# A quantised feed-forward taken chunk by chunk, with its weights turned inside the layer norm ahead of it

## The chip, the cores and the metric

The kernel runs as one program on one core of a Trainium2 chip. The metric is the device time of one execution in microseconds, where less is better. A core has TensorE (matrix products; PE in the rows, PEld for its weight loads), VectorE (DVE), ScalarE (ACT), GpSimd (POOL) and SyncE (SP), which issues the transfers. Each engine runs its own instructions in order, and the engines wait for each other by semaphores.

## The reference, cut to what matters

Two blocks of a perceiver (cross-attention, self-attention, feed-forward) on x of 2 x 256 rows and 256 columns. The changed part is the last: a layer norm and a feed-forward whose weights are quantised to 4 bits in blocks of 32 and whose activations are quantised to 16 bits over the whole tensor. Each `act_qdq` needs the largest absolute value of the entire tensor before its first element can be rounded.

```python
def act_qdq(x):
    scale = jnp.maximum(jnp.max(jnp.abs(x)) / qmax, 1e-12)     # qmax = 32767
    return jnp.clip(jnp.round(x / scale), -qmax - 1.0, qmax) * scale
def fixed_qdq_u16(x):
    scale = 1.0 / 65536.0
    return jnp.clip(jnp.round(x / scale), 0.0, 65535.0) * scale
x = act_qdq(x)                                  # 512 rows x 256
up = act_qdq(x @ lpbq_dequant(w_up).T)          # 512 x 768
gate = act_qdq(x @ lpbq_dequant(w_gate).T)
sig = fixed_qdq_u16(jax.nn.sigmoid(gate))
gate = act_qdq(gate * sig)
o = act_qdq(gate * up)
return o @ lpbq_dequant(w_down).T
# and: x = x + ffn(layernorm(x))
```

## The kernel before

The program is a sequence of blocks. At the end of a block all engines meet, so the next block's first instruction on any engine comes after the previous block's last on every one. Inside a block the order on each engine is the order of the code.

The last two blocks are `layer_norm(chip, "ln5")` and `quantised_ffn`. The layer norm takes statistics of the 512 rows (4 tiles of 128) on VectorE, a power of -0.5 on GpSimd (L155), normalises on VectorE (L147) into `xn`, and turns `xn` on TensorE into `xnT` (2 x 128 partitions x 512 columns), whose halves VectorE and ScalarE (L169) copy out of PSUM.

`quantised_ffn` holds the 768 hidden units as 6 chunks of 128 partitions x 512 columns, side by side as 3072 columns of `gate`, `up` and `sg`. Its work on each engine:

- TensorE turns the three weight matrices (36 transposes of 128 x 128, L2112), then makes 6 gate chunks and 6 up chunks (L2123) in four PSUM banks in turn, and at the end the down product (L2130): 4 tiles of rows, each summed over the 6 chunks before the next tile begins.
- ScalarE copies the turned weights to SBUF (L2138), each chunk of gate and up to SBUF (L2141), then takes the sigmoid of all 3072 columns and its rounding.
- VectorE finds the maxima (L2064 by chunk, L2067 over the six; L2070, L2081, L2087), makes the scales from one column (L2046, L2047), and rounds. Rounding is adding the constant MAGIC = 12582912.0 in float32, and taking it away in a later instruction:

```python
def rounded(t, src, factor):
    link(dve.tensor_scalar(t, src, factor, MAGIC, ALU.mult, ALU.add))                # L2051
    link(dve.tensor_scalar(t, t, MAGIC + QM, MAGIC - QM - 1.0, ALU.min, ALU.max))    # L2052
```

- GpSimd spreads each of the five maxima over the partitions by `partition_all_reduce` (L2102). These five are its only work there. The dequantising of the weights (`DequantisedWeights.work`) was done on GpSimd beside the self-attention before the layer norm.
- SyncE stores the four tiles of the output as VectorE finishes them (L2096).

Names: `f_am` are the maxima per partition, `f_ar` those over all partitions, `f_sc` the scales, `f_rc` their reciprocals, `dq_w` the dequantised weights. `a_all` and `o_all` are two PSUM banks each, `s_all` is four.

Of the kernel before, what the change touches and what calls it, by code (L numbers as in the profile page):

```python
# [10 lines left out]
F32 = mybir.dt.float32  # L11
# [7 lines left out]
P = 128  # L19
# [99 lines left out]
def layer_norm(chip, tag, after=()):  # L119


    nc = chip.nc
    with ExitStack() as scope:
# [6 lines left out]
        with nc.Block() as block:  # L130
# [6 lines left out]
            def _(dve):  # L137
# [20 lines left out]
            def _(pe):  # L158
                pe.wait_ge(xn_done, NT)
# [1791 lines left out]
class DequantisedWeights:  # L1951
# [3 lines left out]
    def __init__(self, chip, tag, scope, mats, outs):  # L1955
# [6 lines left out]
        self.loaded, self.step, self.scaled = (chip.sem(f"{tag}_{n}") for n in ("ld", "step", "scaled"))  # L1962
# [14 lines left out]
    def loads(self, sp):  # L1977
        for i in range(3):
            sp.dma_start(self.flat(i), self.mats[i].rearrange("(o p) c -> p o c", p=P)).then_inc(self.loaded, 16)

# [32 lines left out]
def quantised_ffn(chip, tag, dequantised, upT, gateT, downT, out_dram):  # L2013
# [3 lines left out]
    QM = 32767.0  # L2017
    with ExitStack() as scope:
# [4 lines left out]
        am = chip.sb(f"{tag}_am", [P, 5], F32, scope)  # L2023
        cm = chip.sb(f"{tag}_cm", [P, 2 * I6], F32, scope)
        magic = chip.sb(f"{tag}_magic", [P, 1], F32, scope)
        cmd, magic_set = chip.sem(f"{tag}_cmd"), chip.sem(f"{tag}_magic")
        ar = chip.sb(f"{tag}_ar", [P, 5], F32, scope)
        sc = chip.sb(f"{tag}_sc", [P, 5], F32, scope)
        rc = chip.sb(f"{tag}_rc", [P, 5], F32, scope)
        st, amd, ard, mm, ev, sgd, dn, out, qd = (chip.sem(f"{tag}_{x}") for x in ("st", "amd", "ard", "mm", "ev", "sgd", "dn", "out", "qd"))  # L2030
        stored, tr, tro = chip.sem(f"{tag}_stored"), chip.sem(f"{tag}_tr"), chip.sem(f"{tag}_tro")
        with nc.Block() as block:
            @block.vector
            def _(dve):
                n = 0

                def link(ins):
                    nonlocal n
                    n += 1
                    ins.then_inc(st, 1)  # L2040
                    dve.wait_ge(st, n)

                def scale(i, factor=1.0 / QM):

                    dve.wait_ge(ard, i + 1)
# [3 lines left out]
                def rounded(t, src, factor):  # L2049

                    link(dve.tensor_scalar(t, src, factor, MAGIC, ALU.mult, ALU.add))  # L2051
                    link(dve.tensor_scalar(t, t, MAGIC + QM, MAGIC - QM - 1.0, ALU.min, ALU.max))  # L2052

                def qdq(i, t, src):

                    scale(i)
                    rounded(t, src, rc[:, i:i + 1])
                    dve.tensor_scalar(t, t, MAGIC, sc[:, i:i + 1], ALU.subtract, ALU.mult).then_inc(qd, 1)  # L2058

                def chunk_maxima(first):  # L2060

                    for n in range(first, first + I6):
                        dve.wait_ge(ev, n + 1)
                        dve.tensor_reduce(cm[:, n:n + 1], (gate if n < I6 else up)[:, n % I6, :], AX.X, ALU.max, apply_absolute_value=True).then_inc(cmd, 1)  # L2064
                    dve.wait_ge(cmd, first + I6)
                    i = 1 + first // I6
                    dve.tensor_reduce(am[:, i:i + 1], cm[:, first:first + I6], AX.X, ALU.max).then_inc(amd, 1)  # L2067

                dve.memset(magic[:], MAGIC).then_inc(magic_set, 1)
                dve.tensor_reduce(am[:, 0:1], chip.xnT[:], AX.XY, ALU.max, apply_absolute_value=True).then_inc(amd, 1)  # L2070
# [5 lines left out]
                dve.wait_ge(qd, 3)  # L2076

                dve.wait_ge(sgd, 2)
                link(dve.tensor_scalar(sg[:], sg[:], MAGIC + 65535.0, MAGIC, ALU.min, ALU.max))  # L2079
                link(dve.scalar_tensor_tensor(out=gate[:], in0=sg[:], scalar=MAGIC, in1=gate[:], op0=ALU.subtract, op1=ALU.mult))  # L2080
                dve.tensor_reduce(am[:, 3:4], gate[:], AX.XY, ALU.max, apply_absolute_value=True).then_inc(amd, 1)  # L2081
                scale(3, 2.0 ** -16 / QM)
                link(dve.tensor_scalar(rc[:, 3:4], rc[:, 3:4], 2.0 ** -16, None, ALU.mult))
                rounded(gate[:], gate[:], rc[:, 3:4])

                link(dve.scalar_tensor_tensor(out=gate[:], in0=gate[:], scalar=MAGIC, in1=up[:], op0=ALU.subtract, op1=ALU.mult))
                dve.tensor_reduce(am[:, 4:5], gate[:], AX.XY, ALU.max, apply_absolute_value=True).then_inc(amd, 1)  # L2087
                dve.wait_ge(ard, 5)
# [216 lines left out]
```

## Time and profile before

| | |
|---|---|
| median of 3 runs | 1759.65 us (1758.5 to 1762.81) |
| the profiled execution's time, and its span | 1759.81 us, 1758.0 us |
| TensorE, VectorE, ScalarE, GpSimd busy | 1562.5, 1132.3, 875.0, 685.5 us |
| last layer norm | from 1668.72 to 1675.94 us of the span |
| weight transposes and xq | to 1685.42 us |
| gate and up products | to 1708.0 us |
| element-wise work, TensorE idle | to 1742.80 us |
| down product | to 1755.4 us |
| last sum and store | to 1758.0 us |

The span runs from the first instruction to the end of the last; the time holds some 2 us around it. Busy shares over the span say little about the tail, which is the only part that the change touches; that part is read by its timeline.

### The profile page before, as it was taken

The numbers are of one execution on the slowest core, as the hardware profiler recorded it, in microseconds if no ns is written. First come the engines' busy times: TensorE is split into PE (matmuls) and PEld (weight loads), VectorE is DVE, ScalarE is ACT, GpSimd is POOL, SyncE is SP. The second block draws the span as 40 slices with busy tenths as digits, with TensorE's granted clock in tenths as the row PEclk, the third lists the DMA queues.
The fourth block names the chain that finished last, engine by engine and source line by source line (L and its number), as shares of the span: only waits on it lengthen the run. The fifth ranks groups of instructions, "written<-read, shape, count | busy, mean of one in ns | idle before, by whom it ended". The sixth has DMA issues, their size and how long they took to land. (4 is left out here: it accounts for less than half of the span.)

```text
span 1758.0 us, 42136 instructions
## 1 busy us (share of the span) xinstructions
PE 1562.5 (89%) x15980; PEld 882.6 (50%) x15980; DVE 1132.3 (64%) x1756; ACT 875.0 (50%) x1178; POOL 685.5 (39%) x535
## 2 busy tenths in 40 slices
PE   3999999999499999999777958999999999967772
PEld 1455455455133333333453426777777777753442
DVE  4665665665499999997337747666666666425356
ACT  2555555555167777778251014555555555523440
POOL 2431000000111111111053108999999999933500
PEclk9999999999689999999798969999999999988886
DMA  4787988888432222221300057565546555012000
GB/s 162 199 216 226 223 216 221 222 231 211 146 101 68 65 65 65 65 65 34 153 1 1 1 138 217 152 158 149 146 124 164 145 153 155 27 35 91 1 0 12
DMA packets 178076, 212.14 MB, mean 121 GB/s; under 512 B 57080, under 2 KB 151428, under 8 KB 173342
## 3 DMA queue, kind: packets, MB, share of 16 engines
q1 hardware_dynamic: 177376, 210.37, 43.3%
q8 instruction: 91, 1.49, 0.4%
q14 instruction: 33, 0.27, 0.1%
q10 hardware_dynamic: 576, 0.00, 0.0%
HBM read 122.71 MB, written 87.57 MB: 120 GB/s over the span
## 5 line engine op out<-in xcount | busy, mean ns | idle before, releaser
L1121 POOL TENSOR_TENSOR x_r<-x_p 128x1024 f16<-128x1024 f32 x256 | 479.0, 1893 | 24.0 <-ACT x_p L1097 16.9
L1136 DVE TENSOR_REDUCE x_mx<-a_all 128x2 f32<-128x1024 f32 x249 | 304.9, 1224 | 147.2 <-PE a_all L1020 147.2
L1097 ACT ACTIVATE x_p<-s_all 128x1024 f32<-128x1024 f32 x256 | 248.4, 1022 | 223.1 <-PE s_all L1003 223.1
L702 ACT ACTIVATE x_p<-s_all 128x1024 f32<-128x1024 f32 x256 | 261.0, 1023 | 49.2 <-PE s_all L612 41.9
L757 DVE TENSOR_REDUCE x_mx<-a_all 128x1 f32<-128x512 f32 x352 | 229.9, 684 | 16.7 <-PE o_all L623 8.7
L1003 PE MATMUL s_all<-x_q,x_k 64*128 64x256 f16 x3072 | 210.0, 269 | 0.0
L1038 PEld LDWEIGHTS o_all<-x_v,x_p 128*128 128x128 bf16 x2048 | 178.7, 97 | 40.1 <-issue 40.1
L1038 PE MATMUL o_all<-x_v,x_p 128*128 128x129 f16 x2048 | 197.3, 221 | 0.9 <-POOL x_r L1121 0.9
L1039 PE MATMUL o_all<-x_v,x_r 128*128 128x65 f16 x2048 | 192.5, 193 | 0.0
L1039 PEld LDWEIGHTS o_all<-x_v,x_r 128*128 128x128 f16 x2048 | 180.7, 98 | 0.0
L1003 PEld LDWEIGHTS s_all<-x_q,x_k 64*128 64x128 f16 x3072 | 149.4, 94 | 62.2 <-issue 0.8
L651 PE MATMUL o_all<-x_p,x_vf 128*32 128x256 f32 x2048 | 163.3, 392 | 1.1 <-ACT x_osb L691 1.1
L623 PE MATMUL a_all<-x_k,x_qa 64*128 64x512 f16 x352 | 124.4, 396 | 25.3 <-DMA x_v<-values 22.1
L716 POOL MEMSET x_k<- 128x2048 f16 x2 | 3.6, 1804 | 318.2 <-POOLq L265 318.2
L731 POOL TENSOR_TENSOR x_mcol<-x_nm,x_zero 128x4 f16<-128x4 f32 x32 | 6.8, 213 | 304.8 <-DVE x_nm L764 304.8
L757 DVE TENSOR_REDUCE x_mx<-o_all 128x1 f32<-128x512 f32 x160 | 109.7, 686 | 4.3 <-PE a_all L623 0.5
L1020 PE MATMUL a_all<-x_k,x_q 64*128 64x512 f16 x498 | 97.4, 388 | 13.9 <-DVE x_mx L1136 7.3
L612 PE MATMUL s_all<-x_qb,x_k 64*128 64x256 f16 x1024 | 103.2, 277 | 0.0
L997 PE MATMUL s_all<-x_qm,x_ones 64*128 64x512 f16 x512 | 99.9, 387 | 0.0
L395 DVE TENSOR_TENSOR vst<-a_all,vst 128x512 f16<-128x512 f32 (+1 forms) x96 | 57.9, 603 | 41.4 <-ACT vst L363 40.7
L395 DVE TENSOR_TENSOR vst<-o_all,vst 128x512 f16<-128x512 f32 (+1 forms) x96 | 57.8, 603 | 41.5 <-ACT vst L363 41.0
L612 PEld LDWEIGHTS s_all<-x_qb,x_k 64*128 64x128 f16 x1024 | 30.0, 94 | 104.7 <-issue 82.0
(347 smaller groups left out, 2784.1 us busy)
## 6 DMA issues: line engine op xcount, KB each, us to landing
values<-vst SPq DMA_DIRECT2D x16, 2064.0 KB, 10.3
x_v<-values SPq DMA_DIRECT2D x32, 1032.0 KB, 5.2
keys<-kst SPq DMA_DIRECT2D x32, 1024.0 KB, 6.5
x_k<-keys SPq DMA_DIRECT2D x128, 256.0 KB, 5.1
x_k<-keys SPq DMA_DIRECT2D x192, 64.0 KB, 2.1
values<-vst SPq DMA_DIRECT2D x16, 528.0 KB, 11.5
x_v<-values SPq DMA_DIRECT2D x32, 264.0 KB, 2.6
cf<-in_ctxT SPq DMA_DIRECT2D x16, 512.0 KB, 9.5
```

Of the source, the lines that this page charges most:

```text
L395: dve.tensor_tensor(lo, src, hi, ALU.subtract).then_inc(lo_done, 1)
L612: last = pe.matmul(chip.s_ps[g % 2][:, c * SQ:(c + 1) * SQ], kbuf[w][r, (2 * g + j) * P:(2 * g + j + 1) * P], qb[w][r, :], start=True, sto ...
L623: pe.matmul(bank(place)[:], qa[w][r, qt * P:(qt + 1) * P], kbuf[w][r, c * 512:(c + 1) * 512], start=True, stop=True).then_inc(chunk_ready, 1)
L651: last = pe.matmul(o[32 * c:32 * c + 32, 0:SQ], vf[w][:, kt, :], prob[g % NP][:, c, :], start=(g == 0), stop=(g == GR - 1), skip_group_che ...
L702: act.activation(prob[g % NP][:], chip.s_ps[g % 2][:].rearrange("p (c q) -> p c q", q=SQ), ACT.Exp, scale=hd ** -0.5).then_inc(p_ready, 1)
L757: dve.tensor_reduce(mx[a[1] % 2][:, n // 8, n % 8:n % 8 + 1], bank(place)[:], AX.X, ALU.max).then_inc(chunk_done, 1)
L1003: last = pe.matmul(s[:, c * SQ:(c + 1) * SQ], k[w][kp][r, (2 * g + j) * P:(2 * g + j + 1) * P], q[w][qp][r, :], start=False, stop=(kp == 1 ...
L1038: pe.matmul(o[:, qt * VC:(qt + 1) * VC], hi, v[w][:, kt, :], start=begin, stop=False, skip_group_check=True)
L1039: last = pe.matmul(o[:, qt * VC:qt * VC + 1 + hd], rest[i][:, c, qs], v[w][:, kt, 0:1 + hd], start=False, stop=end, skip_group_check=True)
L1097: act.activation(prob[g % NP][:], chip.s_ps[g % 2][:].rearrange("p (c q) -> p c q", q=SQ), ACT.Exp, scale=hd ** -0.5).then_inc(p_ready, 1)
L1121: pool.tensor_tensor(rest[g % NP][:], prob[g % NP][:], hi, ALU.subtract).then_inc(rest_done, 1)
L1136: dve.tensor_reduce(mx[a[1] % 2][:, n // 4, 2 * (n % 4):2 * (n % 4) + 2], chunk_banks(u, g)[:, :].rearrange("p (h c) -> p h c", h=2), AX.X ...
```

## The change

The changed feed-forward works on chunks of 512 columns throughout:

- The weight transposes and their copies move into the layer norm (`turned`), ahead of the transposes of `xn` on TensorE and of the copy of `xnT` on ScalarE. GpSimd calls one idle all-reduce and then that of the first maximum there (`scales`); this maximum is now taken of `xn`, before it is turned.
- The gate chunks stay in PSUM (banks 0 to 5, the up chunks in banks 6, 7 and 0 to 3). VectorE takes maxima there, and ScalarE's rounding (an Identity activation with scale `rc` and bias MAGIC) brings them to SBUF.
- ScalarE does all rounding of gate, silu, up and the product, by chunks; the clips of the five `act_qdq` go (only the sigmoid's upper one stays). VectorE subtracts MAGIC and multiplies. For chunks 0 to 3 ScalarE also subtracts MAGIC from the rounded sigmoid, for 4 and 5 VectorE.
- The down product runs over chunks outside and over row tiles inside, so it needs one chunk at a time.

```diff
@@ layer_norm, VectorE, GpSimd, TensorE, ScalarE
+                if scales is not None:
+                    dve.wait_ge(xn_done, NT)
+                    dve.tensor_reduce(scales.am[:, 0:1], chip.xn[:], AX.XY, ALU.max, apply_absolute_value=True).then_inc(scales.found, 1)
...
                 pool.tensor_tensor(rs[:], ve[:], chip.half[:, 0:NT], ALU.pow).then_inc(rstd, 1)
+                if scales is not None:
+                    pool.partition_all_reduce(scales.idle[:], chip.half[:, 0:1], P, bass.bass_isa.ReduceOp.absmax)
+                    scales.over_rows(pool, 0)
...
+                if turned is not None:
+                    turned.turn(pe)
                 pe.wait_ge(xn_done, NT)
...
+                if turned is not None:
+                    turned.keep(act)
                 act.wait_ge(tr, 2)
@@ quantised_ffn, VectorE
-                qdq(0, xq[:], chip.xnT[:])
-                chunk_maxima(0)
-                qdq(1, gate[:], gate[:])
-                chunk_maxima(I6)
-                qdq(2, up[:], up[:])
...
+                scale(0)
+                for k in range(KT):
+                    link(dve.tensor_scalar(xq[:, k, :], chip.xnT[:, k, :], rc[:, 0:1], MAGIC, ALU.mult, ALU.add))
+                    dve.tensor_scalar(xq[:, k, :], xq[:, k, :], MAGIC, sc[:, 0:1], ALU.subtract, ALU.mult).then_inc(x_done, 1)
+                for m in range(I6):
+                    dve.wait_ge(gate_ready, m + 1)
+                    chunk(0, m, gate_bank[m])
+                largest(1, 0, I6)
+                scale(1)
+                dve.sem_inc(scale_done, 1)
+                for m in range(I6):
+                    gate_back(m)
+                    if m in (1, 3, 5):
+                        up_max(m // 2)
+                silu_max(0)
+                up_max(3)
+                silu_chunk(0)
+                for m in range(1, 4):
+                    silu_max(m)
+                    if m < 3:
+                        up_max(3 + m)
+                    silu_chunk(m)
+                    if m == 2:
+                        largest(2, 1, 2 * I6 + 3)
+                scale(2)
+                dve.sem_inc(scale_done, 1)
+                for m in range(4, I6):
+                    whole(m)
+                    silu_max(m)
+                    silu_chunk(m)
+                largest(3, 2, 3 * I6)
+                for m in range(4):
+                    up_back(m)
...
+                for m in range(4, I6):
+                    up_back(m)
+                product(0)
+                for m in range(1, I6):
+                    product(m)
+                    product_chunk(m - 1)
+                product_chunk(I6 - 1)
+                largest(4, 3, 4 * I6)
...
+                link(dve.tensor_scalar(gate[:, 0, :], gate[:, 0, :], rc[:, 4:5], MAGIC, ALU.mult, ALU.add))
+                for m in range(I6):
+                    if m:
+                        dve.wait_ge(down_round, m)
+                    dve.tensor_scalar(gate[:, m, :], gate[:, m, :], MAGIC, sc[:, 4:5], ALU.subtract, ALU.mult).then_inc(down_done, 1)
@@ quantised_ffn, TensorE: the down product
+                for k in range(I6):
+                    pe.wait_ge(down_done, k + 1)
+                    for t in range(NT):
                         last = pe.matmul(chip.banks[t][:, 0:D], gate[:, k, t * P:(t + 1) * P], downT[:, k, :],
@@ quantised_ffn, ScalarE
-                act.activation(sg[:], gate[:], ACT.Sigmoid).then_inc(sgd, 1)
...
+                def rounded(out, src, i, done):
+                    act.activation(out, src, ACT.Identity, bias=magic[:, 0:1], scale=rc[:, i:i + 1]).then_inc(done, 1)
...
+                act.activation(warm[:], magic[:, 0:1], ACT.Sigmoid)
+                act.wait_ge(scale_done, 1)
+                for m in range(I6):
+                    rounded(gate[:, m, :], gate_bank[m], 1, gate_round)
+                for m in range(I6):
+                    sigmoid(m)
+                    sigmoid_round(m)
+                    if m < 4:
+                        sigmoid_whole(m)
+                act.wait_ge(scale_done, 2)
+                for m in range(I6):
+                    rounded(up[:, m, :], up_bank[m], 2, up_round)
+                act.wait_ge(scale_done, 3)
+                for m in range(I6):
+                    rounded(silu[:, m, :], silu[:, m, :], 3, silu_round)
+                act.wait_ge(scale_done, 4)
+                for m in range(1, I6):
+                    rounded(gate[:, m, :], gate[:, m, :], 4, down_round)
```

GpSimd in the last two blocks, before: the power of the layer norm, a branch into the feed-forward's block, and there the all-reduces, the first with an instruction without operands ahead of it (both print as ISA).

```order
L155 TENSOR_TENSOR ln_rs<-ln_ve,half 128x4
L130 UNCONDITIONAL_BRANCH
L2098 UNCONDITIONAL_BRANCH
L2102 ISA
L2102 ISA f_ar<-f_am 128x1 x5
```

The same place of the changed kernel:

```order
L157 TENSOR_TENSOR ln_rs<-ln_ve,half 128x4
L159 ISA
L159 ISA f_idle<-half 128x1
L2046 ISA f_ar<-f_am 128x1
L129 UNCONDITIONAL_BRANCH
L2194 UNCONDITIONAL_BRANCH
L2046 ISA f_ar<-f_am 128x1 x4
```

The instruction without operands and the first all-reduce of a maximum now stand ahead of the branch, inside the layer norm.

VectorE from the silu product to the last scale, before:

```order
L2080 SCALAR_TENSOR_TENSOR f_gate<-f_sg,f_gate 128x3072
L2081 TENSOR_REDUCE f_am<-f_gate 128x1
L2046 TENSOR_SCALAR f_sc<-f_ar 128x1
L2047 RECIPROCAL f_rc<-f_sc 128x1
L2083 TENSOR_SCALAR f_rc<-f_rc 128x1
L2051 TENSOR_SCALAR f_gate<-f_gate,f_rc 128x3072
L2052 TENSOR_SCALAR f_gate<-f_gate 128x3072
L2086 SCALAR_TENSOR_TENSOR f_gate<-f_gate,f_up 128x3072
L2087 TENSOR_REDUCE f_am<-f_gate 128x1
```

VectorE of the changed kernel, from chunk 5 of silu to the second chunk of the product (the maxima of `f_cm` are over one chunk):

```order
L2114 TENSOR_SCALAR f_sg<-f_sg 128x512
L2109 SCALAR_TENSOR_TENSOR f_silu<-f_sg,f_gate 128x512
L2092 TENSOR_REDUCE f_cm<-f_silu 128x1
L2096 TENSOR_REDUCE f_am<-f_cm 128x1
L2122 TENSOR_SCALAR f_up<-f_up,f_sc 128x512 x4
L2087 TENSOR_SCALAR f_sc<-f_ar 128x1
L2088 RECIPROCAL f_rc<-f_sc 128x1
L2170 TENSOR_SCALAR f_rc<-f_rc 128x1
L2122 TENSOR_SCALAR f_up<-f_up,f_sc 128x512 x2
L2127 SCALAR_TENSOR_TENSOR f_gate<-f_silu,f_up 128x512 x2
L2092 TENSOR_REDUCE f_cm<-f_gate 128x1
```

The passes L2051 and L2052 over 3072 columns are gone from VectorE, four of the six instructions that scale `up` back stand between a maximum and its scale, and products and maxima alternate by chunk.

## Rows read from the trace of the kernel before

**Rows 1.** The page: head.

```profile
span 1758.0 us, 42136 instructions
```

**Rows 2.** The chain over 1660 to 1758 us: shares by line; pieces (start, us, what).

```profile
by line: issue 17.1%; PE a_all L2123 12.5%; PE o_all L2123 10.5%; PE a_all L2130 7.6%; PE o_all L2130 5.3%; DVE f_gate L2080 3.4%; DVE f_am L2081 3.4%; DVE f_up L2051 1.9%; DVE f_up L2058 1.9%; DVE f_gate L2051 1.9%; DVE f_gate L2093 1.9%; 
...
1742.80 7.43 PE a_all L2130 x24
1750.22 5.19 PE o_all L2130 x24
```

**Rows 3.** Timeline, last layer norm (start us, us, engine, line, operation).

```profile
1668.72 1.40 DVE L139 BATCH_NORM_STATS2 ln_st<-x 128x6 f32<-128x256 f32 x4 [0.51 <-PEq L1180]
...
1670.82 1.04 POOL L155 TENSOR_TENSOR ln_rs<-ln_ve,half 128x4 f32<-128x4 f32 x1 [12.21 <-DVE ln_ve L144]
1671.89 1.38 DVE L147 TENSOR_SCALAR xn<-x,ln_mv,ln_rs 128x256 f32<-128x256 f32 x4 [1.15 <-POOL ln_rs L155]
...
1675.34 0.60 ACT L169 ACTIVATE xnT<-a_all 128x512 f32<-128x512 f32 x1 [11.43 <-PE a_all L162]
```

**Rows 4.** Timeline, start of the feed-forward.

```profile
1676.24 6.97 PE L2112 MATMUL s_all<-ident,dq_w 128*128 128x128 f32 x36 [0.94 <-PEq L130]
...
1682.17 0.41 POOL L2102 PARTITION_ALL_REDUCE f_ar<-f_am  x1 [10.31 <-issue]
...
1683.00 0.75 DVE L2051 TENSOR_SCALAR f_xq<-xnT,f_rc 128x1024 f32<-128x1024 f32 x1
...
1684.52 0.76 DVE L2058 TENSOR_SCALAR f_xq<-f_xq,f_sc 128x1024 f32<-128x1024 f32 x1
...
1685.42 5.37 PE L2123 MATMUL a_all<-f_xq,gateT 128*128 128x512 f32 x8 [2.21 <-DVE f_xq L2058]
```

**Rows 5.** Timeline, the last gate chunk, its scale, the last up chunk.

```profile
1697.69 0.60 ACT L2141 ACTIVATE f_gate<-a_all 128x512 f32<-128x512 f32 x1 [1.12 <-PE a_all L2123]
...
1699.04 0.16 DVE L2067 TENSOR_REDUCE f_am<-f_cm 128x1 f32<-128x6 f32 x1
...
1699.88 0.16 DVE L2047 RECIPROCAL f_rc<-f_sc 128x1 f32<-128x1 f32 x1
...
1707.99 0.60 ACT L2141 ACTIVATE f_up<-o_all 128x512 f32<-128x512 f32 x1 [1.12 <-PE o_all L2123]
```

**Rows 6.** Timeline, VectorE to the end.

```profile
1705.46 3.84 DVE L2064 TENSOR_REDUCE f_cm<-f_up 128x1 f32<-128x512 f32 x6
...
1717.67 3.36 DVE L2080 SCALAR_TENSOR_TENSOR f_gate<-f_sg,f_gate 128x3072 f32<-128x3072 f32 x1
...
1732.52 3.35 DVE L2087 TENSOR_REDUCE f_am<-f_gate 128x1 f32<-128x3072 f32 x1
...
1736.98 0.16 DVE L2091 TENSOR_TENSOR f_rc<-f_rc,f_sc 128x1 f32<-128x1 f32 x1
...
1755.44 0.42 DVE L2096 TENSOR_TENSOR x<-o_all,x 128x256 f32<-128x256 f32 x1 [2.17 <-PE o_all L2130]
```

**Rows 7.** Groups by form: line, operation, count, busy us, mean ns, idle before.

```profile
L2064 DVE TENSOR_REDUCE f_cm<-f_gate 128x1 f32<-128x512 f32 x6 | 4.1, 686 | 9.6 <-ACT f_gate L2141 9.6
L2141 ACT ACTIVATE f_gate<-a_all 128x512 f32<-128x512 f32 x4 | 2.4, 597 | 8.6 <-PE a_all L2123 8.6
L361 ACT ACTIVATE kst<-o_all,bk 128x512 f16<-128x512 f32 x64 | 43.9, 686 | 34.9 <-PE o_all L336 34.9
L2093 DVE TENSOR_SCALAR f_gate<-f_gate,f_sc 128x3072 f32<-128x3072 f32 x1 | 1.8, 1820 | 0.0
```

**Rows 8.** Timeline of ScalarE in the last self-attention.

```profile
1607.81 0.59 ACT L1573 ACTIVATE s_hi<-a_all 128x512 f16<-128x512 f32 x1
1608.28 0.60 ACT L1577 ACTIVATE s_lo<-a_all 128x512 f16<-128x512 f32 x1
```

**Rows 9.** Busy time by stretch; the number after POOL's is TensorE's granted clock.

```profile
1685.40:1688.80 3.40, 3.38 (x4) 1.50 (x5) 0.00 (x0) 0.00 (x0) 0.00 (x0) 0.50 0.00 0
1688.80:1698.00 9.20, 9.20 (x23) 4.07 (x22) 3.43 (x5) 3.30 (x6) 0.00 (x0) 1.00 0.00 0
```

More of the change, by code:

```diff
@@ L1979, in loads, with turn, keep @@
             sp.dma_start(self.flat(i), self.mats[i].rearrange("(o p) c -> p o c", p=P)).then_inc(self.loaded, 16)
+    def turn(self, pe):
+        for n, (_i, _dst, srcs) in enumerate(self.jobs):
+            if n >= 4:
+                pe.wait_ge(self.kept, n - 3)
+            for a, src in enumerate(srcs):
+                last = pe.transpose(self.chip.banks[4 + n % 4][:, a * P:(a + 1) * P], src, self.chip.ident[:])
+            last.then_inc(self.tr, 1)
+    def keep(self, act):
+        for n, (_i, dst, srcs) in enumerate(self.jobs):
+            act.wait_ge(self.tr, n + 1)
+            act.activation(dst, self.chip.banks[4 + n % 4][:, 0:len(srcs) * P], ACT.Copy).then_inc(self.kept, 1)
     def scales(self, dve, i):
@@ L2017, in quantised_ffn @@
     QM = 32767.0
+    gate_bank = [chip.banks[m] for m in range(I6)]
+    up_bank = [chip.banks[(I6 + m) % 8] for m in range(I6)]
     with ExitStack() as scope:
@@ L2054, in qdq @@
[L2054 to L2067, printed above, removed]
@@ L2080, in _, with chunk, largest @@
[L2080 to L2081 removed]
+                def chunk(part, m, src):
+                    c = part * I6 + m
+                    dve.tensor_reduce(cm[:, c:c + 1], src, AX.X, ALU.max, apply_absolute_value=True).then_inc(chunk_max, 1)
+                def largest(i, part, total):
+                    dve.wait_ge(chunk_max, total)
+                    dve.tensor_reduce(am[:, i:i + 1], cm[:, part * I6:(part + 1) * I6], AX.X, ALU.max).then_inc(found, 1)
@@ new lines, in up_max, with gate_back, silu_max @@
+                def up_max(m):
+                    dve.wait_ge(up_ready, m + 1)
+                    chunk(1, m, up_bank[m])
+                def gate_back(m):
+                    dve.wait_ge(gate_round, m + 1)
+                    dve.tensor_scalar(gate[:, m, :], gate[:, m, :], MAGIC, sc[:, 1:2], ALU.subtract, ALU.mult).then_inc(gate_done, 1)
+                def silu_max(m):
+                    dve.wait_ge(sg_whole, m + 1)
+                    dve.wait_ge(gate_done, m + 1)
+                    dve.scalar_tensor_tensor(out=silu[:, m, :], in0=sg[:, m, :], scalar=65535.0, in1=gate[:, m, :],
+                                             op0=ALU.min, op1=ALU.mult).then_inc(silu_done, 1)
@@ new lines, in whole, with silu_chunk, up_back @@
+                def whole(m):
+                    dve.wait_ge(sg_round, m + 1)
+                    dve.tensor_scalar(sg[:, m, :], sg[:, m, :], MAGIC, None, ALU.subtract).then_inc(sg_whole, 1)
+                def silu_chunk(m):
+                    dve.wait_ge(silu_done, m + 1)
+                    chunk(2, m, silu[:, m, :])
+                def up_back(m):
+                    dve.wait_ge(up_round, m + 1)
+                    dve.tensor_scalar(up[:, m, :], up[:, m, :], MAGIC, sc[:, 2:3], ALU.subtract, ALU.mult).then_inc(up_done, 1)
@@ new lines, in product, with product_chunk @@
+                def product(m):
+                    dve.wait_ge(silu_round, m + 1)
+                    dve.wait_ge(up_done, m + 1)
+                    dve.scalar_tensor_tensor(out=gate[:, m, :], in0=silu[:, m, :], scalar=MAGIC, in1=up[:, m, :],
+                                             op0=ALU.subtract, op1=ALU.mult).then_inc(product_done, 1)
+                def product_chunk(m):
+                    dve.wait_ge(product_done, m + 1)
+                    chunk(3, m, gate[:, m, :])
+                dve.memset(magic[:, 0:1], MAGIC).then_inc(magic_set, 1)
@@ new lines, in _ @@
+                for m in range(I6):
+                    for k in range(KT):
+                        if m == 0:
+                            pe.wait_ge(x_done, k + 1)
+                        last = pe.matmul(gate_bank[m], gateT[:, k, m * P:(m + 1) * P], xq[:, k, :], start=(k == 0), stop=(k == KT - 1))
+                    last.then_inc(gate_ready, 1)
+                for m in range(I6):
+                    if m >= 2:
+                        pe.wait_ge(gate_round, m - 1)
+                    for k in range(KT):
+                        last = pe.matmul(up_bank[m], upT[:, k, m * P:(m + 1) * P], xq[:, k, :], start=(k == 0), stop=(k == KT - 1))
+                    last.then_inc(up_ready, 1)
```

118 lines of the change are left out of this document (51 added, 67 removed).

## The prediction

> **What bounds the kernel now.** I read the timeline first, to find where the changed code runs, then the chain of waits over it, then groups and stretches for prices. Nothing before the last layer norm is touched: the change can only move the time from about 1668.7 us to the end of the span at 1758.0 [rows 1]. In that tail almost nothing overlaps. The chain [rows 2] goes over long pieces of one engine after another: the two products with the gate and up weights (L2123, the parts named a_all and o_all), the down product (L2130) in two pieces of 7.43 and 5.19 us, and between them VectorE instructions over all 3072 columns. The reader should see in [rows 3, 4] that the layer norm ends with ScalarE's copy at 1675.34 + 0.60 = 1675.94, and that the first gate product starts only at 1685.42. GpSimd's first all-reduce (L2102) began at 1682.17, though its data came from a reduction that needed 1.2 us of the block: its idle time is put down to "issue", no engine. So something that belongs to this first call takes 1682.17 - 1676.24 = 5.93 us from the opening of the block, and xq waits for it. From the last gate chunk to its scale [rows 5] it is an eviction, a reduction and the all-reduce; then VectorE works alone until the down product at 1742.80, and TensorE stands still from 1708.0.
>
> **The prices of one chunk of 512 columns.** VectorE's reduction takes 0.686 us for 512 columns [rows 7] and 3.36 us for 3072 [rows 6], so a column costs 1.04 ns and the two-input instruction (3.36 us for 3072) comes to 0.69 us too. Six reductions in a row take 3.84 us [rows 6], 0.64 us each. A one-input instruction costs 0.752 us at 1024 columns [rows 4] and 1.82 us at 3072 [rows 7]: 0.52 ns a column, 0.48 us at 512, and I take 0.43 in a row. ScalarE takes 0.597 us, or 0.686 with a column operand [rows 7]; instructions that don't wait for each other start 0.47 us apart [rows 8], 0.12 less than they last; I take 0.11 less, so 0.58 us in a row with a column operand. A dependent instruction on another of these engines starts 0.03 us after its producer (1670.82 + 1.04 to 1671.89, [rows 3]), and TensorE 0.14 us after VectorE (1684.52 + 0.76 to 1685.42, [rows 4]).
>
> **Step 1, the start of the gate product.** The 36 weight transposes and their evictions move into the layer norm, ahead of xn's own eight on TensorE and ahead of xnT's copy on ScalarE. The first all-reduce, with an idle one before it, moves there as well, behind the power at L155. Three ends compete. GpSimd: the power ends at 1670.82 + 1.04 = 1671.86 [rows 3]; + 5.93, and two all-reduces of 0.41 [rows 4], gives 1678.61. TensorE and ScalarE: 36 transposes took 6.97 us [rows 4]; from 1668.72 they end at 1675.7, eight more at the same rate 1677.2, a copy of 0.60 gives 1677.9. VectorE has 1.2 us of reduction more behind 1673.3 and is done before that. So GpSimd ends the block, 2.7 us later than now. Then 0.30 us to the next block (1675.94 to 1676.24), 0.1 for two one-column memsets, 0.38 for two one-column operations, 0.48 + 0.03 + 0.48 for the first half of xq, 0.14 to TensorE: 1680.5. Before, 1685.42: **4.9 us** gained. The second half of xq comes 0.9 us later, while TensorE has 1.7 us or more of work on the first. TensorE's clock was 0.50 of full speed, 1.2 GHz, in the first 3.4 us of the product and 2.4 GHz after it [rows 9]; before the product it had stood still for 2.2 us. Now it stands still longer, so I keep the slow start.
>
> **Step 2, the gate scale.** Chunks stay in PSUM and VectorE reduces them there, so the eviction between product and reduction falls away: 1697.69 + 0.60 before the reduction starts [rows 5]. **0.65 us** with its gap.
>
> **Step 3, from the gate scale to the down product.** It took 1742.80 - 1700.04 = 42.76 us [rows 2, 5]. Now, with t = 0 at the gate scale:
> - To the up scale. ScalarE rounds six chunks, 0.03 + 0.69 + 5 x 0.58 = 3.62, then per chunk sigmoid, rounding and subtraction, each dependent: 0.60 + 0.69 + 0.69 + 0.06 = 2.04, and 1.93 in a row. The first whole chunk is there at 5.55. VectorE then has, per chunk, a product with the gate, an up maximum and a silu maximum: 3 x 0.64 = 1.93, the same pace. Three such rounds to 11.4, the small maximum 0.16, another product and maximum 1.4, two one-column operations 0.34: 13.25. The last up chunk is no limit: six chunks of (1707.99 - 1697.69)/6 = 1.72 us behind the gate's put it at 8.6, and its maximum has its turn at 10.1.
> - To the silu scale. Chunks 4 and 5 each 0.42 + 0.69 + 0.69 with gaps, 3.67; the small maximum 0.19; four one-input instructions 1.72; three one-column ones 0.5: 6.0.
> - To the last scale. 0.03 + 0.69 for ScalarE's first rounded chunk, then six products and six maxima on VectorE at 0.64, 7.7; with the small maximum and the same handing over as now, (1736.98 + 0.16) - (1732.52 + 3.35) = 1.27 [rows 6]: 10.0.
> - To TensorE: 0.48 + 0.48 + gaps + 0.14 = 1.2, one chunk instead of three passes.
> Together 30.4. I add 0.2 for four separate semaphore increments that VectorE now issues behind the scales (estimate, 0.05 each). **12.2 us** gained. Why it shrinks: four rounding passes over 3072 columns (L2051) leave VectorE for ScalarE, and four clipping passes (L2052) are gone.
>
> Here the Trainium skill speaks against the change: Perfetto Trace Analysis, Optimizing Scalar/DVE Operations, says that every VectorE or ScalarE instruction pays a fixed access cost, about 60 ns on VectorE from SBUF, so larger operations are better where the engine is full. The row bears out the direction with a larger size: six pieces in 3.84 us against one of 3.36 is 0.10 us for each extra instruction [rows 6]. By the page's figure the some 33 chunk instructions of this step on VectorE would take 1.3 us less than in my sum (estimate); I keep the row's.
>
> **Step 4, the end.** 48 products in 1755.44 - 1742.80 = 12.64 us [rows 2, 6], the slow clock at their start included. Chunk by chunk they can't be faster than now, but VectorE's chunks come every 0.48 to 0.58 us and TensorE needs at least 12.64/6 x 0.8 = 1.7 for one: no wait. The four sums now come in the last 1.3 us rather than one every 2.6, and so do the four stores: I take 0.3 us lost, between 0 (the last store starts no later) and 1.0.
>
> Sum: 4.9 + 0.65 + 12.2 - 0.3 = 17.4 us. The span becomes 1740.6; the profiled execution took 1759.81 around a span of 1758.0, so 1742.4, and as its time is within 0.2 us of the median of the runs, 1742.4 is the forecast, 1.0% faster.
>
> **Bounds.** If nothing pipelines (0.69 for each ScalarE and VectorE chunk instruction, dependent or not), step 3 takes 2.2 us more. If GpSimd's first call needs 1.2 us more, that goes to the block's end whole. If TensorE starts the gate product at 2.4 GHz, 1.9 us less (1685.42 + 5.4 for what takes 3.43 later). With the scatter of the three runs around their median, -1.2 to +3.2 us, I get 1739 to 1747.5; that is the forecast's own range too, and it holds the two milder rivals.
>
> **Rivals.**
> - ScalarE and VectorE wait for each other at each chunk, and the handing over costs more than 0.03 us; some 35 handings over in step 3 at 0.14 us, TensorE's price, would add 3.9 us: 1746.3. For it: the chain of now has few handings over, so 0.03 rests on few rows. Against it: those rows are of the same two engines. 13 in 100.
> - The layer norm takes it back. If the transposes hold up xn's, or the first call comes later, the block ends at 1681 and step 1 gives 2.5: 1744.8. Against it: 0.7 us of slack between the two ends. 8 in 100.
> - The change doesn't do what it says: the tail shrinks, but the other 1669 us of the span, whose code is the same, grow by 0.7% or more, as their instructions lie elsewhere in memory. No row shows such a thing. The time would be within 5.3 us of now (0.3%, about what a measurement of this kernel can tell from no change): 1757. 2 in 100.
> - Slower. TensorE stays at 1.2 GHz through gate, up and down products. The last up chunk then comes at 12 x 3.43 = 41.2 us behind the start, 17 us after VectorE's turn for it, and the down product takes 4 x 5.19 = 20.8 (24 of its 48 products took 5.19 at the end [rows 2]) instead of 12.6, 8.2 more: 1742.4 + 25 = 1767.6. From 17.4 us of lateness on it decides. For it: the clock was at 0.50 at the start of the same product, and TensorE stands still longer before it. Against it: the same unbroken row of products brought the clock to 1.00 after 3.4 us [rows 9]. 2 in 100. The Trainium skill, TensorE: Matmul & The Clock Gate, in its part on oscillation, describes bursts divided by waits that each start at the slow clock; by it the down product, now six bursts, would suffer if they were apart, and here none waits.
>
> The forecast's own mechanism has 75 in 100. Of all cases 96 in 100 are faster by over 0.3%, 2 within, 2 slower.
>
> **What the new profile would show.** In the layer norm GpSimd's last all-reduce ends at 1678.6 and is the last instruction of the block; the gate product starts at 1680.5; 14.0 us later ScalarE's first rounding; scales at +13.3, +6.0, +10.0 us; the down product at about 1724.9; ScalarE's instructions 0.58 us apart. VectorE and ScalarE both busy over 85% in between. Wrong would be: a start of the gate product after 1682, one-input instructions of over 0.55 us beside ScalarE, or gaps over 0.1 us at each chunk.

## The result, and the profile after

The changed kernel takes 1741.18 us (median of 4 runs, 1739.34 to 1743.06) against 1760.52 us for the kernel before beside it (4 runs, 1758.5 to 1762.81): a ratio of 0.9895, 95% interval 0.9882 to 0.9908, or 16.2 to 20.8 us. The forecast was 1742.4.

The profiled execution has a span of 1737.6 us. Its timeline in the last layer norm and at the opening of the feed-forward answers to [rows 3, 4] (start us, us, engine, line, operation):

```profile
1665.14 1.41 DVE L138 BATCH_NORM_STATS2 ln_st<-x 128x6 f32<-128x256 f32 x4 [0.51 <-PEq L1189]
1665.14 4.88 PE L1996 MATMUL s_all<-ident,dq_w 128*128 128x128 f32 x36 [0.98 <-PEq L1189]
...
1667.25 1.04 POOL L157 TENSOR_TENSOR ln_rs<-ln_ve,half 128x4 f32<-128x4 f32 x1 [11.90 <-DVE ln_ve L143]
...
1670.94 0.60 ACT L178 ACTIVATE xnT<-a_all 128x512 f32<-128x512 f32 x1 [0.30 <-PE a_all L169]
1674.22 0.41 POOL L159 PARTITION_ALL_REDUCE f_idle<-half  x1 [5.94 <-issue]
1674.55 0.43 POOL L2046 PARTITION_ALL_REDUCE f_ar<-f_am  x1
1675.29 1.28 ACT L2240 ACT_TABLE_LOAD   x1 [3.76 <-PEq L129]
...
1676.84 6.01 PE L2205 MATMUL a_all<-f_xq,gateT 128*128 128x512 f32 x8 [5.94 <-DVE f_xq L2139]
```

GpSimd's idle call starts 5.94 us after the end of the power (1667.25 + 1.04), idle time that the profile puts down to "issue", and the block ends with the all-reduce at 1674.98, while ScalarE's last copy was done at 1671.54: 3.4 us of the block are the first call alone. The statistics begin at 1665.14, 3.58 us earlier in the span than before, in code that is the same; the experiments come back to this. So the stages are compared by their distances, not by their places.

VectorE and ScalarE from the gate scale on, and the end (answering to [rows 5, 6]):

```profile
1691.31 0.16 DVE L2088 RECIPROCAL f_rc<-f_sc 128x1 f32<-128x1 f32 x1
1691.57 1.45 ACT L2225 ACTIVATE f_gate<-a_all,f_magic,f_rc 128x512 f32<-128x512 f32 x2 [14.78 <-DVEq L2145]
...
1705.35 0.16 DVE L2088 RECIPROCAL f_rc<-f_sc 128x1 f32<-128x1 f32 x1
...
1709.42 1.67 DVE L2122 TENSOR_SCALAR f_up<-f_up,f_sc 128x512 f32<-128x512 f32 x4
...
1711.18 0.16 DVE L2088 RECIPROCAL f_rc<-f_sc 128x1 f32<-128x1 f32 x1
...
1711.63 4.34 ACT L2225 ACTIVATE f_silu<-f_silu,f_magic,f_rc 128x512 f32<-128x512 f32 x6 [1.26 <-DVEq L2171]
...
1721.15 0.16 DVE L2183 TENSOR_TENSOR f_rc<-f_rc,f_sc 128x1 f32<-128x1 f32 x1
...
1722.61 2.05 PE L2217 MATMUL a_all<-downT,f_gate 128*128 128x256 f32 x4 [22.59 <-DVE f_gate L2189]
...
1734.44 0.85 DVE L2192 TENSOR_TENSOR x<-o_all,x 128x256 f32<-128x256 f32 x2
```

Busy time by stretch of the changed kernel, answering to [rows 9] (PE, PEld, DVE, ACT, POOL, then the granted clock):

```profile
1691.50:1722.60 31.10, 8.52 (x20) 3.44 (x19) 27.45 (x59) 24.01 (x36) 1.85 (x3) 0.72 0.00 1
1676.84:1680.80 3.96, 3.96 (x5) 1.85 (x6) 0.97 (x3) 0.00 (x0) 0.00 (x0) 0.50 0.00 0
1680.80:1690.00 9.20, 9.20 (x22) 3.94 (x21) 3.57 (x6) 0.00 (x0) 0.00 (x0) 0.96 0.00 0
```

Between the gate scale and the down product VectorE is busy 88% and ScalarE 77% of the time. The gate product begins at 1.2 GHz again (0.50). The mean of 0.96 in the next stretch says that the rise came some 0.7 us into it, so the slow start lasts 4.6 us instead of 3.4. Groups by form, answering to [rows 7]:

```profile
L2225 ACT ACTIVATE f_silu<-f_silu,f_magic,f_rc 128x512 f32<-128x512 f32 x6 | 4.3, 802 | 1.3 <-DVEq L2171 1.3
L2233 ACT ACTIVATE f_sg<-f_sg,f_magic 128x512 f32<-128x512 f32 x6 | 4.3, 722 | 0.2
L2109 DVE SCALAR_TENSOR_TENSOR f_silu<-f_sg,f_gate 128x512 f32<-128x512 f32 x6 | 4.2, 692 | 1.2 <-ACT f_sg L2237 0.8
```

The distances, in us, one profiled execution each (the gate scale is the end of its reciprocal; the down product runs to the end of the span):

| stage | before | forecast | after |
|---|---|---|---|
| first statistics to the gate product's start | 16.70 | 11.8 | 11.70 |
| gate product's start to the gate scale | 14.62 | 13.97 | 14.63 |
| gate scale to the down product's start | 42.76 | 30.6 | 31.14 |
| down product's start to the end | 15.20 | 15.5 | 14.99 |
| sum | 89.28 | 71.9 | 72.46 |

### The profile page after: what moved, and what is told of

It is laid out like the page before. It is cut to its first block and busy times, and to the rows that moved or that the text cites. A ratio compares the mean times of both kernels' runs of the same rounds, so it can differ in the third digit from the quotient of the medians.

```text
span 1737.6 us, 42209 instructions
## 1 busy us (share of the span) xinstructions
PE 1554.7 (89%) x15980; PEld 876.2 (50%) x15980; DVE 1120.5 (64%) x1789; ACT 888.9 (51%) x1204; POOL 687.4 (40%) x536
## 5 line engine op out<-in xcount | busy, mean ns | idle before, releaser
L1029 PE MATMUL a_all<-x_k,x_q 64*128 64x512 f16 x498 | 97.4, 388 | 14.3 <-DVE x_mx L1145 7.3
```

## The experiments

All were profiled and timed beside the kernel before, the first four together, the next four together, the last by itself. "Tail" is the distance from the last layer norm's first statistics to the end of the span, in the profiled execution.

| kernel | median us | ratio to before | statistics start at | to gate product | to gate scale | to down product | to end | tail |
|---|---|---|---|---|---|---|---|---|
| a_turn_only | 1759.60 | 1.0009 | 1665.80 | 15.78 | 15.77 | 42.76 | 15.69 | 90.00 |
| b_first_reduce_only | 1759.26 | 0.9994 | 1667.20 | 16.87 | 12.94 | 42.77 | 15.82 | 88.40 |
| c_down_by_tile | 1748.30 | 0.9937 | 1666.44 | 11.65 | 14.67 | 34.22 | 15.02 | 75.56 |
| d_no_early_table | 1745.55 | 0.9929 | 1665.81 | 11.44 | 14.91 | 32.65 | 16.09 | 75.09 |
| after_again | 1743.31 | 0.9903 | 1670.78 | 11.61 | 14.83 | 31.14 | 15.14 | 72.72 |
| e_clock_kept | 1738.77 | 0.9879 | 1670.24 | 11.61 | 12.38 | 31.62 | 13.35 | 68.96 |
| f_early_first_call | 1741.30 | 0.9896 | 1673.30 | 8.97 | 12.38 | 31.14 | 14.91 | 67.40 |
| g_both | 1734.52 | 0.9856 | 1668.63 | 9.21 | 12.38 | 31.16 | 13.32 | 66.07 |
| h_chunk3_on_vector | 1735.52 | 0.9872 | 1667.32 | 9.21 | 12.39 | 31.46 | 13.42 | 66.48 |

**Each move into the layer norm alone.** Both start from the kernel before. a_turn_only takes the transposes and their copies into the layer norm:

```diff
             def _(pe):
+                if turned is not None:
+                    turned.turn(pe)
                 pe.wait_ge(xn_done, NT)
...
             def _(act):
+                if turned is not None:
+                    turned.keep(act)
```

> The kernel before, with only the weight transposes and their copies moved into the layer norm. My theory: the start of the gate product was bound by GpSimd's first all-reduce (5.93 us from the block's opening), so moving the transposes alone gives nothing: the gate product starts 13.6 us after the end of the power on GpSimd, as before, and the time is 1760.5 us, within 1 us. Rival: the transposes (6.97 us) bound it: the gate product starts some 4 us earlier, 1756.

b_first_reduce_only takes the idle all-reduce and the first maximum there:

```diff
                 pool.tensor_tensor(rs[:], ve[:], chip.half[:, 0:NT], ALU.pow).then_inc(rstd, 1)
+                if scales is not None:
+                    pool.partition_all_reduce(scales.idle[:], chip.half[:, 0:1], P, bass.bass_isa.ReduceOp.absmax)
+                    scales.over_rows(pool, 0)
```

> The kernel before, with only the idle all-reduce and that of the first maximum moved into the layer norm; the transposes stay in the feed-forward. My theory: the block of the layer norm ends 2.7 us later and the transposes then take their 7.0 us, so the gate product starts 14.1 us after the power instead of 13.6: 1761, within 1 us of before or a little slower; the two moves pay only together (5.0 us). Rival: the first call was the only bound, and this move alone brings the 5 us: 1755.5.

Neither is told from before: ratios 1.0009 (0.9996 to 1.0021) and 0.9994 (0.9982 to 1.0006). The timeline of a_turn_only shows what holds its gate product up:

```profile
1671.60 0.60 ACT L173 ACTIVATE xnT<-a_all 128x512 f32<-128x512 f32 x1 [0.29 <-PE a_all L164]
...
1678.43 0.41 POOL L2120 PARTITION_ALL_REDUCE f_ar<-f_am  x1 [9.49 <-issue]
...
1681.58 6.51 PE L2134 MATMUL a_all<-f_xq,gateT 128*128 128x512 f32 x8 [10.02 <-DVE f_xq L2076]
```

The layer norm is over at 1672.20 and all weights are turned, but the first all-reduce starts 6.2 us later, and TensorE waits for xq. In b_first_reduce_only the all-reduce is out of the way, and the transposes are in it:

```profile
1676.58 0.43 POOL L2029 PARTITION_ALL_REDUCE f_ar<-f_am  x1
...
1677.36 6.04 PE L2126 MATMUL s_all<-ident,dq_w 128*128 128x128 f32 x36 [3.58 <-PEq L130]
...
1684.07 3.70 PE L2137 MATMUL a_all<-f_xq,gateT 128*128 128x512 f32 x8 [0.67 <-ACT downT L2152]
```

Here the product's releaser is ScalarE's copy of the turned weights. The start comes 0.9 us earlier than before in one and 0.2 later in the other; in the changed kernel it is 5.0 us earlier. Two works of 6 to 7 us stood side by side, and each covered the other. Not all of the 5.0 us is the two moves, though. In b_first_reduce_only xq, still made whole and with its clip, is ready 12.85 us after the first statistics:

```profile
1679.30 0.75 DVE L2074 TENSOR_SCALAR f_xq<-f_xq,f_sc 128x1024 f32<-128x1024 f32 x1
```

With 0.14 us to TensorE the two moves alone would start the product at 13.0 (estimate), 3.7 us earlier than before. The other 1.3 us come from xq in halves and without its clip. No run has the two moves alone.

A detail in the same rows: the first eight matmul records take 6.51 us where TensorE had waited 10.02 us, and 3.70 us where it came straight from the transposes. In before it was 5.37 us, in the changed kernel 6.01.

**The order of the down product.** c_down_by_tile is the changed kernel with

```diff
-                for k in range(I6):
-                    pe.wait_ge(down_done, k + 1)
-                    for t in range(NT):
+                pe.wait_ge(down_done, I6)
+                for t in range(NT):
+                    for k in range(I6):
```

> The changed kernel, with the down product again over row tiles outside and chunks inside, waiting for all six chunks. My theory: it starts when the sixth chunk is ready, 2.95 us later than in the changed kernel, less 0.3 us that the spread stores give back: 1741.2 + 2.7 = 1743.9. Rival: the product's slow start at 1.2 GHz hides the order, and the time stays at 1741.2.

```profile
1726.98 7.22 PE L2217 MATMUL a_all<-downT,f_gate 128*128 128x256 f32 x24 [25.67 <-DVE f_gate L2189]
...
1739.42 0.42 DVE L2192 TENSOR_TENSOR x<-o_all,x 128x256 f32<-128x256 f32 x1 [2.17 <-PE o_all L2217]
```

The down product starts 34.22 us after the gate scale instead of 31.14, 3.1 us later. From its start to the end it takes 15.02 us, as in the changed kernel (14.99), but that sum hides two small differences. From the end of the last addition to the end of the span it takes 2.16 us (1742.0 - 1739.84) against 2.31 in the changed kernel (1737.6 - 1735.29); over all profiles it is 2.07 to 2.16 us where the tiles end 2.6 us apart and 2.31 to 2.36 where they end together. So the spread stores do give back 0.15 us, half of what was expected. And the product's slow start lasted 3.7 us here against 3.3. The tail is 3.1 us longer (2.8 against after_again). The rival falls. The medians differ by 5 us (from after_again) to 7, more than the tail of the one profiled execution explains; the rest may lie ahead of the layer norm, where nothing was changed, but only one execution was profiled, the fastest of the four.

**The table load.** d_no_early_table leaves out the one-column sigmoid:

```diff
-                act.activation(warm[:], magic[:, 0:1], ACT.Sigmoid)
```

> The changed kernel without the one-column sigmoid at the opening of the feed-forward. My theory: the table load of 1.28 us then falls between ScalarE's rounding of the gate and its first sigmoid, on the path to the up scale, which ScalarE paces: 1741.2 + 1.3 = 1742.5. Rival: VectorE paces that stretch and hides it: 1741.2.

ScalarE's timeline shows the load where it was expected:

```profile
1694.98 1.46 ACT L2225 ACTIVATE f_gate<-s_all,f_magic,f_rc 128x512 f32<-128x512 f32 x2
1696.46 1.28 ACT L2229 ACT_TABLE_LOAD   x1
1697.76 0.63 ACT L2229 ACTIVATE f_sg<-f_gate 128x512 f32<-128x512 f32 x1
```

Gate scale to down product is 32.65 instead of 31.14, 1.5 us more, the load with what it displaces. The rest of the tail's 2.6 us is not the load's: 0.3 in the gate product and 1.1 from the down product on, whose slow start lasted 5.3 us here and 3.3 in the changed kernel.

**The changed kernel again.** No edit.

> The changed kernel once more, unaltered, as the measure for the three kernels run beside it. My theory: the last layer norm's first statistics to the end of the span take 72.5 us again, within 1.5 us for where TensorE's clock rises; the time of the part ahead of it, whose code is that of before, scatters by some us from execution to execution (it was 1668.7 and 1665.1 us in the two first profiles). Rival: the part ahead is shorter in the changed kernel for good, by some 2 us.

Every distance in the tail repeats within 0.2 us; the statistics begin 5.6 us later than in its first profile. Over all eleven profiles, whose code is the same up to there but for GpSimd's first call in three of them, that start lies between 1665.1 and 1673.3 us. The rival, a part ahead that is shorter for good, is not borne out. Two stretches ahead of the tail, the first pair of the first profile, the second of after_again:

```profile
480.00:500.00 20.00, 17.95 (x71) 4.56 (x70) 19.52 (x35) 6.31 (x7) 3.07 (x6) 0.57 0.33 88
500.00:520.00 20.00, 19.73 (x220) 7.42 (x216) 18.55 (x35) 15.85 (x18) 1.53 (x3) 1.00 0.45 131
```

```profile
480.00:500.00 20.00, 18.19 (x63) 4.67 (x67) 19.52 (x35) 6.42 (x7) 2.81 (x6) 0.50 0.32 88
500.00:520.00 20.00, 19.73 (x208) 6.98 (x200) 17.32 (x31) 14.31 (x17) 1.80 (x4) 0.92 0.44 130
```

TensorE is busy for the same share of both, but its clock rises later in the second, and it gets through 271 records there instead of 291. By the two means the lower clock lasts 6.0 us longer in the second, which is worth 3.0 us at most of the 5.6 (estimate). So it goes with a part of the longer time; that it is the cause of the scatter was not shown. Of the four executions timed beside after_again the median is 15.8 us below before's (14.2 to 20.1 us by the interval, 0.9886 to 0.9919), against 19.3 the first time.

**The clock.** e_clock_kept adds idle transposes that nobody reads:

```diff
+                    pe.wait_ge(turned.kept, len(turned.jobs))
+                    for n in range(32):
+                        pe.transpose(chip.banks[4 + n % 4][:, 0:P], chip.ident[:], chip.ident[:])
...
+                for n in range(12):
+                    pe.transpose(chip.banks[7][:, 0:P], chip.ident[:], chip.ident[:])
                 for m in range(I6):
...
                 pe.wait_ge(up_round, I6)
+                for n in range(90):
+                    pe.transpose(chip.banks[7][:, 0:P], chip.ident[:], chip.ident[:])
```

> The changed kernel with idle transposes on TensorE: 32 behind those of xn, 12 ahead of the gate product, 90 ahead of the down product, into PSUM banks that nobody reads. My theory: both products then start at 2.4 GHz. From the gate product's start to the gate scale 12.0 instead of 14.6 us, from the down product's start to its last sum 10.4 instead of 12.3: 72.5 - 4.5 = 68.0 us from the first statistics to the end, and 4.5 us less in all. Rival: VectorE's maxima and the weight loads set the pace of the gate product, or the idle transposes delay it, and less than 1 us comes of it.

```profile
1681.85 3.76 PE L2211 MATMUL a_all<-f_xq,gateT 128*128 128x512 f32 x8
...
1713.16 12.85 PE L2221 MATMUL s_all<-ident 128*128 128x128 f32 x90 [10.39 <-ACT f_up L2233]
...
1725.85 1.03 PE L2225 MATMUL a_all<-downT,f_gate 128*128 128x256 f32 x4
```

The first eight gate records take 3.76 us, and the first four of the down product 1.03 instead of 2.05. The two stages shrink by 2.2 and 1.6 us. But the 90 transposes began at 1.2 GHz themselves (0.50 from 1713.2 to 1718) and end at 1726.01, so the down product starts 0.5 us late. The tail is 68.96: 3.5 to 3.8 us less, 4.5 expected.

**The first call ahead of the layer norm.** f_early_first_call:

```diff
+    def work(self, pool):
+        pool.partition_all_reduce(self.idle2[:], self.half[:, 0:1], P, bass.bass_isa.ReduceOp.absmax)
...
-                rows_project(chip, "o3", att, D, wo, add_to_x(chip))
+                rows_project(chip, "o3", att, D, wo, add_to_x(chip), after=[scales])
... layer norm, with scales: instead of the power on GpSimd
+                    dve.wait_ge(root, 1)
+                    dve.reciprocal(rs[:], ve[:]).then_inc(rstd, 1)
...
+                        act.activation(ve[:], ve[:], ACT.Sqrt).then_inc(root, 1)
+                    act.activation(scales.idle[:], chip.half[:, 0:1], ACT.Sqrt, scale=-1.0)
+                    turned.keep(act, 4, take_root)
```

> The changed kernel with GpSimd's idle all-reduce moved into the output projection of the self-attention, ahead of the layer norm, and the power taken off GpSimd: a square root on ScalarE (its table loaded ahead of the weight copies) and a reciprocal on VectorE. My theory: GpSimd's first call (5.94 us) bounds the layer norm's end in the changed kernel; without it ScalarE's copy of xnT does, some 2.8 us earlier, so the gate product starts 8.9 us after the first statistics instead of 11.7; and as TensorE has stood still for less time its clock may still be at 2.4 GHz, up to 2.6 us more. 67 to 70 us from the first statistics to the end. Rival: the projection's block ends later by the first call, or the square root's table load holds up the copies, and nothing is won.

```profile
1670.91 0.41 POOL L2062 PARTITION_ALL_REDUCE f_idle<-half  x1 [9.06 <-issue]
1673.30 1.41 DVE L139 BATCH_NORM_STATS2 ln_st<-x 128x6 f32<-128x256 f32 x4 [0.52 <-PEq L1199]
...
1679.36 0.36 POOL L2066 PARTITION_ALL_REDUCE f_ar<-f_am  x1 [8.04 <-DVE f_am L156]
...
1679.85 0.60 ACT L188 ACTIVATE xnT<-a_all 128x512 f32<-128x512 f32 x1 [0.29 <-PE a_all L175]
...
1682.27 3.76 PE L2225 MATMUL a_all<-f_xq,gateT 128*128 128x512 f32 x8 [2.45 <-DVE f_xq L2159]
```

The first call is over before the statistics, and the layer norm now ends with ScalarE's copy at 1680.45. The gate product starts at 8.97 us instead of 11.6, and its first eight records take 3.76 us without a single idle transpose. The wait ahead of it was 2.45 us. That alone does not explain the fast start, as before waited less (2.21 us, [rows 4]) and began slowly. What differs is what TensorE did ahead of the wait: in before it turned the weights at 1.2 GHz for 5.8 us and at 2.4 for only 1.2,

```profile
1676.20:1682.00 5.80, 5.76 (x27) 5.79 (x28) 1.22 (x2) 3.41 (x8) 0.00 (x0) 0.50 0.01 3
1682.00:1683.20 1.20, 1.20 (x11) 0.92 (x9) 0.52 (x3) 1.20 (x6) 0.41 (x1) 0.99 0.00 0
```

while here its granted clock was 1.00 from 1671.1 on, through all 44 transposes. Which of this decides was not tested. The tail is 67.40, 5.1 to 5.3 us less. The median is only 2.0 us below that of after_again. In the profiled execution the part ahead was the longest of all (1673.30), and that isn't the early call: g_both and h_chunk3_on_vector have it too, with 1668.63 and 1667.32.

**Both.** g_both is f_early_first_call with 8, 8 and 90 idle transposes in the three places.

> Both of the two last: first call ahead of the layer norm, and idle transposes (8 behind xn's, 8 ahead of the gate product, 90 ahead of the down product). My theory: the gains add except for the gate product's clock, which counts once: gate product at 8.9 us, 72.5 - 2.8 - 4.5 = 65.2 us from the first statistics to the end, 7.3 us less than the changed kernel. Rival: as in the two kernels by themselves.

The tail is 66.07, against 65.2 expected: the gate product starts 0.3 us later than I took (9.21), its stage is 12.38 and not 12.0, and from the down product on it is 13.32 where 13.1 was meant. The idle transposes on the gate side bought nothing here: the stage is 12.38 us without them as well (f_early_first_call), and the product starts 0.24 us later with them. Only the 90 ahead of the down product pay. The median, 1734.52, is 8.8 us below after_again's on the same chip, and the ratio to before is 0.9856 (0.9840 to 0.9873).

**One more chunk for VectorE.** h_chunk3_on_vector is g_both with

```diff
-                    if m < 4:
+                    if m < 3:
                         sigmoid_whole(m)
...
                 for m in range(1, 4):
+                    if m == 3:
+                        whole(m)
                     silu_max(m)
```

> The kernel with both (g_both), and the subtraction that makes chunk 3 of the rounded sigmoid whole done by VectorE instead of ScalarE. My theory: ScalarE paces the stretch from the gate scale to the up scale (2.03 us a chunk), VectorE follows with less; a 0.72 us instruction off ScalarE and a 0.43 us one on VectorE brings the up scale 0.3 us earlier, and VectorE's wait of 0.57 us for the last rounded sigmoid goes too: 65.2 us from the first statistics to the end instead of 66.1. Rival: VectorE is the pace, and its 0.43 us more makes it longer.

My theory fell. The up scale comes 14.45 us after the gate scale instead of 14.04, 0.4 us later, which is the instruction added to VectorE:

```profile
1700.46 0.67 DVE L2116 TENSOR_REDUCE f_cm<-f_silu 128x1 f32<-128x512 f32 x1
1701.16 0.16 DVE L2120 TENSOR_REDUCE f_am<-f_cm 128x1 f32<-128x6 f32 x1
1701.24 0.42 DVE L2138 TENSOR_SCALAR f_sg<-f_sg 128x512 f32<-128x512 f32 x1
1701.69 0.69 DVE L2133 SCALAR_TENSOR_TENSOR f_silu<-f_sg,f_gate 128x512 f32<-128x512 f32 x1
```

VectorE has no wait around it: at the end of this stretch it is the pace, though ScalarE sets it at the start, as the table load showed. The tail is 66.48 against 66.07, one profile each; the ratios to before, 0.9872 (0.9851 to 0.9892) and 0.9856 (0.9840 to 0.9873), don't tell the two kernels apart.

## Why the prediction was right

The time was forecast at 1742.4 and is 1741.18; the tail was to give 17.4 us and gave 89.28 - 72.46 = 16.8. The interval of the whole, 16.2 to 20.8 us, holds both. That the time itself came within 1.2 us is partly luck. The two profiled spans differ by 20.4 us, and 3.6 of them lie ahead of the tail, in code that is the same and whose length scatters by 8 us between profiles; the changed kernel's second set of executions has its median at 1743.31. What the forecast is right about is the tail, and there its errors partly cancel.

- **Step 1**, forecast 4.9 us: 5.0. That the first all-reduce and the transposes each cover the other, and that GpSimd then ends the block, is shown by a_turn_only, b_first_reduce_only and f_early_first_call: each move alone gives nothing that can be told, and with the call gone the block ends with ScalarE. That some 1.3 of the 5.0 us are xq's (a term of the forecast's sum too) is read from rows. The transposes were quicker than I took them: begun right behind the projection, at 2.4 GHz, they left 3.4 us of slack and not 0.7.
- **Step 2**, forecast 0.65 us: nothing. The reduction does follow the product at once, which saves the 0.65 us, but the product lost 0.64: I kept its slow start at the old length, and its first eight records took 6.01 us for what took 5.37, as the clock stayed at 1.2 GHz for 4.6 us and not 3.4. That it is the clock is shown by e_clock_kept, where the stage is 12.38 us. Why the slow start was longer is not shown: in the four profiles of this stage with waits of 5.67 to 5.94 us it lasts 4.6 to 5.3 us, longest after the shortest wait. The Trainium skill, TensorE: Matmul & The Clock Gate, under Why this matters for your kernels, says that an idle gap between bursts of products, if it is long enough, puts the next start back to the slow clock. The trace agrees in part: the same eight records take 6.51 us after a wait of 10.02 and 3.70 after 0.67, but 5.37 after 2.21 and 3.76 after 2.45, so the length of the wait alone doesn't decide.
- **Step 3**, forecast 12.2 us: 11.6. The structure held stage by stage: gate scale to up scale 14.04 (13.25 forecast), to the silu scale 6.0 (6.0), to the last scale 9.8 (10.0), to TensorE 1.3 (1.2 and the increments). The price that was off is ScalarE's: an instruction with scale and bias from a column lasts 0.77 to 0.80 us, with a bias column from SBUF 0.72, not 0.69, and six independent roundings take 4.34 us, 0.71 apart, not 0.58. It delays the up scale by 0.8 us. VectorE's price was off the other way, by a wrong reading: six reductions in 3.84 us [rows 6] were taken as 0.64 each and 0.10 us for each extra instruction, but the sixth began only at 1708.62 (the chain of before has it as the piece `1708.62 0.70 DVE f_cm L2064`), when ScalarE's last copy was done (1707.99 + 0.60, [rows 5]); the first five start 0.59 us apart. In the changed kernel the products and maxima of the last scale start 0.60 apart, so an extra instruction costs 0.06 us, the lower of the two figures that the forecast set side by side. (Its terms for the last scale add up to 9.85 and not 10.0.) The eight passes that left VectorE had taken 14.3 us in before (4 x 1.82 of rounding, 4 x 1.76 of clipping), and c_down_by_tile gives 3.1 us to the order of the down product; no run takes back the roundings or the clips one by one, so how the rest divides between them is read from the rows, not tested.
- **Step 4**, forecast a loss of 0.3 us: a gain of 0.2. The stores behind each other do cost something, 0.17 us (2.31 against 2.14 from the last addition's end), but the product itself took 12.22 us instead of 12.60, as its slow start was 3.3 us long instead of 4.1. That is scatter and not the change: it was 5.3 in d_no_early_table.
- The handing over between ScalarE and VectorE was 0.02 to 0.05 us, about as taken: the rival of 0.14 falls. So does the rival of a layer norm that takes the gain back, and that of a TensorE at 1.2 GHz to the end: its clock rose 4.6 us after the gate product's start. The rival of a part ahead that grows falls too: it is 1665.1 to 1673.3 us long in the changed kernels and 1665.8 to 1668.7 in before, a_turn_only and b_first_reduce_only, with no growth of 0.7%.
- That VectorE and ScalarE would both be busy over 85% was wrong for ScalarE (77%): it waits for the scales, 5.43 us for the last.

What stays open is what moves the part ahead of the tail by up to 8 us between executions of the same code; the clock's rise in the two stretches shown goes with a part of it, and no run separates it. What sets the length of TensorE's slow start (4.6 to 5.7 us for the gate product where the weights are turned in the layer norm and it begins slowly) stays open too.

## What to carry to other kernels

When two works of like length stand side by side ahead of the same instruction, moving one gives nothing and moving both gives all; price the moves together, and test each alone. A first call of an instruction on GpSimd that shows as idle time put down to "issue" is work like any other: begin it a block earlier, where that engine is free. Work that is cut into chunks so that two engines can share it is worth its extra instructions when the handing over is short, but a wait that it leaves on TensorE can be paid a second time in the clock (here 6.01 us for what takes 3.76). Before a price is taken from a row of several like instructions, look whether one of them waited.

## What the runs showed of the hardware that I had not expected

- ScalarE's instructions with both scale and bias from a column cost more than plain copies: from SBUF six start 0.71 us apart and last 0.80 each, where copies of the same size from PSUM started 0.47 apart and lasted 0.60 [rows 8].
- Idle transposes ahead of a product gave it the granted clock of 2.4 GHz, by keeping it ahead of the gate product (3.76 us for eight records instead of 6.01 to 6.51) and by raising it ahead of the down product (1.03 instead of 2.05 for its first four).
- GpSimd's first all-reduce in the layer norm started 5.68 to 5.94 us after the end of the power in all five kernels that have it behind the power, though its data (a constant) were there all along.
